# A vision tower on one core: attention steps in another order, two FFN slots interleaved, all high parts on ScalarE

## The reference

```python
    hx = _layernorm(x, ln_g, ln_b)
    q, k, v = (hx @ Wq), (hx @ Wk), (hx @ Wv)             # 2 heads of 64
    q = _l2norm(q) * scale * qn_g;  k = _l2norm(k) * scale * kn_g
    scores = jnp.einsum('bhqd,bhkd->bhqk', q, k) * dh ** (-0.5)      # causal
    attn = jax.nn.softmax(scores, axis=-1)
    y = (attn @ v) @ Wo
    gate = jax.nn.softmax(y @ gate_W + gate_b, axis=-1)
    hid = jax.nn.gelu(jnp.einsum('bnd,edf->bnef', y, W1) + b1)       # E = 8, FF = 512
    eo = jnp.einsum('bnef,efd->bned', hid, W2) + b2
    out = jnp.einsum('bned,bne->bnd', eo, gate)
```

## Time and profile before

| | |
|---|---|
| three runs, median (lowest to highest) | 1539.38 us (1537.39 to 1545.45) |
| the profiled execution | 1542.88 us, its span 1540.7 us |
| mean granted TensorE clock | 0.986 of full |
| PE busy | 1462.2 us, 95% |
| DVE busy | 1238.6 us, 80% |
| ACT busy | 1082.8 us, 70% |
| POOL busy | 329.9 us, 21% |

### The profile page before, as it was taken

One profiled execution on the slowest core, in us unless ns is written; L12 is line 12 of the kernel. 1 busy time (PEld: TensorE's weight loads), 2 busy tenths in 40 slices (PEclk: granted clock), 3 DMA queues, 4 the chain that ended last, 5 costly groups with the idle time before them and its releaser, 6 DMA issues.

```text
span 1540.7 us, 31400 instructions
## 1 busy us (share of the span) xinstructions
PE 1462.2 (95%) x10991; PEld 994.6 (65%) x10991; DVE 1238.6 (80%) x2585; ACT 1082.8 (70%) x1861; POOL 329.9 (21%) x337
## 2 busy tenths in 40 slices
PE   7898889999999999999999999999999999999998
PEld 4554556666666666666666666666666666666665
DVE  6768798878888888888888788888788888887765
ACT  5232667777777777786777777786777777777766
POOL 1135044030121313130211313130211213130101
PEclk9998899999999999999999999999999999999979
DMA  7866053333324242434233242433333242433324
GB/s 241 202 155 140 2 164 46 101 45 100 45 61 84 27 115 39 103 42 104 42 92 53 32 113 36 109 45 100 42 94 50 47 95 34 110 44 102 54 92 55
DMA packets 40340, 125.55 MB, mean 81 GB/s; under 512 B 5744, under 2 KB 5744, under 8 KB 38128
## 3 DMA queue, kind: packets, MB, share of 16 engines
q0 software_dynamic: 22464, 55.81, 25.7%
q1 hardware_dynamic: 17696, 69.28, 12.7%
q10 hardware_dynamic: 144, 0.01, 0.0%
HBM read 68.98 MB, written 50.48 MB: 78 GB/s over the span
## 4 chain that ended last, share of the span: by engine, by line
PE 59%; DVE 22%; issue 9%; ACT 7%; DMA 2%; DVEq 1%; ACTq 0%; POOLq 0%
PE pair L1009 18%; PE pair L1028 18%; PE pair L779 6%; DVE area L1434 4%; PE pair L766 4%; DVE area L1447 3%; ACT area L645 3%; PE pair L943 3%; PE pair L931 3%; DVE mx L1332 2%; ACT area L640 2%; DVE root_t L1267 2%; PE pair L807 2%; DVE area L1347 2%; PE pair L950 2%
## 5 line engine op out<-in xcount | busy, mean ns | idle before, releaser
L640 ACT ACTIVATE area<-pair,pack_b_sb 128x680 f32<-128x680 f32 x512 | 422.6, 828 | 208.1 <-PE pair L1009 206.3
L1434 DVE TENSOR_TENSOR area<-area 128x680 f16<-128x680 f32 x512 | 458.2, 898 | 128.7 <-ACT area L645 124.1
L1028 PE MATMUL pair<-area,ws 128*128 128x340 f16 x3072 | 527.9, 308 | 15.7 <-DVE area L1447 11.8
L1009 PE MATMUL pair<-area,ws 128*128 128x340 f16 x3072 | 530.2, 308 | 1.4
L1028 PEld LDWEIGHTS pair<-area,ws 128*128 128x128 f16 x3072 | 286.4, 98 | 178.9 <-DVE area L1447 44.0
L1009 PEld LDWEIGHTS pair<-area,ws 128*128 128x128 f16 x3072 | 295.3, 98 | 144.1 <-ACT area L645 3.6
L475 POOL DMA_DIRECT2D tower_out<-area x128 | 109.9, 859 | 1030.7 <-DVE area L1447 979.7
L645 ACT ACTIVATE area<-pair,pack_b_sb 128x680 f16<-128x680 f32 x384 | 316.6, 825 | 0.0
L1447 DVE SCALAR_TENSOR_TENSOR area<-pair,pack_b_sb,area 128x340 f32<-128x340 f32 x256 | 133.6, 562 | 9.4 <-PE pair L1028 9.2
L604 ACT ACTIVATE area<-pair,nbias,root 85x85 f32<-85x85 f32 (+1 forms) x256 | 112.4, 463 | 4.2 <-DVE nbias L1335 4.2
L766 PE MATMUL pair<-area,pack_a_sb 128*128 128x392 f32 (+1 forms) x260 | 92.7, 499 | 17.5 <-DVE area L1254 14.4
(11 more groups left out here) (222 smaller groups left out, 1772.8 us busy)
## 6 DMA issues: line engine op xcount, KB each, us to landing
tower_out<-area POOLq DMA_DIRECT2D x128, 340.0 KB, 4.6
area<-gate_scratch SPq DMA_DIRECT2D x16, 1360.0 KB, 10.0
area<-gate_scratch SPq DMA_DIRECT2D x16, 1020.0 KB, 7.3
area<-cells SPq DMA_DIRECT2D x16, 392.0 KB, 4.9
area<-cells POOLq DMA_DIRECT2D x14, 392.0 KB, 6.5
area<-area POOLq DMA_DIRECT2D x14, 392.0 KB, 4.3
tower_out<-ht SPq DMA_DIRECT2D x16, 340.0 KB, 2.3
area<-gate_scratch SPq DMA_DIRECT2D x16, 340.0 KB, 4.7
```

The lines of the kernel that those rows point to most:

```text
L640: nc.scalar.activation(two(hid[slot % NHID]), halves(hid_ps[slot % 2]), ACT.Gelu_apprx_tanh, bias=col(COL_B1 + slot)).then_inc(hid_ready, 1)
L1009: last = mm(hid_ps[slot % 2][:, j, 0:TH], lhs[:, w], rhs[:, j * TH:(j + 1) * TH], start=(i == 0), stop=(i == 2))
L1028: last = mm(eo_ps[:, j, 0:TH], lhs[:, w], rhs[:, j * TH:(j + 1) * TH], start=(m % CH == 0 and i == 0), stop=(m % CH == CH - 1 and i == 2))
L1434: v.tensor_tensor(hl[slot % NPART], hid[slot % NHID], hh[slot % NPART], ALU.subtract).then_inc(hlo_ready, 1)
```

## The change

- `DVE_HI = ()`: the high part of every slot is made by the second GELU pass on ScalarE. VectorE casts none. The semaphore counts follow, and TensorE's slot n + 2 now always waits for the second pass (`hidden_read`).
- FFN slots 0 and 1: their W1 matmuls are issued bank by bank, that is, logits of half 0, half 0 of slot 0, half 0 of slot 1, logits of half 1, half 1 of slot 0, half 1 of slot 1. Slot 1's own place in the order is then empty.
- Attention, VectorE: normalise 0, values 0, normalise 1, values 1, turned 0, normalise 2, turned 1, normalise 3, turned 2, turned 3.
- Attention, TensorE: channel 2 stands between the transposes of images 0 and 1, channel 3 before the transposes of image 3, and the first projection before the weighing of image 2.

```diff
+DVE_HI = ()
...
         def hi_on_act(slot):
 
-            return slot % CH > 0
+            return slot not in DVE_HI
...
+            def hidden_read(g, slot):
+
+                if hi_on_act(slot):
+                    pe.wait_ge(hhi_act, his(g, slot + 1))
+                else:
+                    pe.wait_ge(hid_ready, g * SLOTS + slot + 1)
...
                 turn_probs(g, 0)
+                graph_of(2)
                 turn_probs(g, 1)
-                graph_of(2)
                 weigh(g, 0)
                 turn_probs(g, 2)
                 weigh(g, 1)
+                graph_of(3)
                 turn_probs(g, 3)
-                graph_of(3)
+                project(g, 0)
                 weigh(g, 2)
-                project(g, 0)
                 weigh(g, 3)
...
+            def expert_half(slot, j):
+                w = slice(slot * D, (slot + 1) * D)
+                for i, (lhs, rhs) in enumerate(((w1h, yh), (w1h, yl), (w1l, yh))):
+                    last = mm(hid_ps[slot % 2][:, j, 0:TH], lhs[:, w], rhs[:, j * TH:(j + 1) * TH],
+                              start=(i == 0), stop=(i == 2))
+                return last
+
             def experts_in(g, slot):
 
-                n = g * SLOTS + slot
-                if slot >= 2 and hi_on_act(slot - 2):
-                    pe.wait_ge(hhi_act, his(g, slot - 1))
-                elif slot >= 2:
-                    pe.wait_ge(hid_ready, n - 1)
-                if slot % CH == 0:
-                    pe.wait_ge(wlo_done, 2 * (slot // CH) + 1)
-                w = slice(slot * D, (slot + 1) * D)
-                for j in range(2):
-                    if slot == 0:
+                if slot == 0:
+                    pe.wait_ge(wlo_done, 1)
+                    for j in range(2):
                         logits(g, j)
-                    for i, (lhs, rhs) in enumerate(((w1h, yh), (w1h, yl), (w1l, yh))):
-                        last = mm(hid_ps[slot % 2][:, j, 0:TH], lhs[:, w], rhs[:, j * TH:(j + 1) * TH],
-                                  start=(i == 0), stop=(i == 2))
-                last.then_inc(hid_ps_ready, 1)
+                        for n in range(2):
+                            last = expert_half(n, j)
+                            if j == 1:
+                                last.then_inc(hid_ps_ready, 1)
+                if slot >= 2:
+                    hidden_read(g, slot - 2)
+                    if slot % CH == 0:
+                        pe.wait_ge(wlo_done, 2 * (slot // CH) + 1)
+                    expert_half(slot, 0)
+                    expert_half(slot, 1).then_inc(hid_ps_ready, 1)
...
                 normalise(g, 0)
+                values_out(g, 0)
                 normalise(g, 1)
-                values_out(g, 0)
                 values_out(g, 1)
+                turned(g, 0)
                 normalise(g, 2)
-                turned(g, 0)
                 turned(g, 1)
```

More of the change, by code:

```diff
@@ L303, in hi_on_act @@
         def hi_on_act(slot):
-            return slot % CH > 0
+            return slot not in DVE_HI
         def his(g, slot):
-            return g * (SLOTS - E) + len([n for n in range(slot) if hi_on_act(n)])
+            return g * (SLOTS - len(DVE_HI)) + len([n for n in range(slot) if hi_on_act(n)])
         def steps_in(slots, slot):
@@ L906, in scores @@
                 if later:
-                    pe.wait_ge(hhi_act, his(g, 0) - 1 + m)
+                    hidden_read(g - 1, SLOTS - 2 + m)
                 elif m == 1:
@@ L1432, in experts @@
                     v.tensor_copy(hh[slot % NPART], hid[slot % NHID]).then_inc(hhi_dve, 1)
-                    dve.wait_ge(hhi_dve, g * E + slot // CH + 1)
+                    dve.wait_ge(hhi_dve, g * len(DVE_HI) + DVE_HI.index(slot) + 1)
                 v.tensor_tensor(hl[slot % NPART], hid[slot % NHID], hh[slot % NPART], ALU.subtract).then_inc(hlo_ready, 1)
```

## The result

| | before | after |
|---|---|---|
| median of the runs of this comparison | 1540.45 us | 1551.8 us (1550.74 to 1556.33, 5 runs) |
| ratio to before, 95% interval | | 1.0071 (1.0049 to 1.0092) |
| the profiled execution, its span | 1542.88, 1540.7 us | 1556.33, 1554.5 us |
| mean granted clock | 0.986 | 0.960 |
| mean of the 13 like groups (2 to 14) | 85.76 us | 86.33 us |

The change made the kernel 0.7% slower; 1.4% faster was forecast. The page shows the engine mix moving as forecast, though by less than the summed instructions (66.8 and 105.6 us): VectorE is busy 55 us less and ScalarE 85 us more. TensorE is busier by 20 us with the same 10991 matmuls. That is the first sign: the same matmuls took longer.

A forecast was written before the change was run, and what follows sets the result against it. TensorE was taken as the bound, busy 1462.2 of 1540.7 us. Like groups 10.8, slot 12 gaps 5.7, first group 1.8 and last 3 sum to 21.3: 1539.38 to 1518, range 1512 to 1525, with rivals (1) and (4) 1508 to 1532.

The forecast's parts named there:

- rival (3): TensorE's pause of about 1.1 us before slot 2 lowers its clock: +3 us, 1542 to 1600; chance 0.03.
- The interleaving: FFN slots 0 and 1 issued bank by bank: fills 0.43 us of TensorE standing, by itself worth nothing.
- The walk of waits: Both queues stepped through one steady group: attention 0.64 us earlier, new wait of 0.35 before transposes 2, slot 2 at 879.70.
- 0.77 + 0.44 = 1.21: Per like group: 0.77 us ahead by W2 slot 4, plus the 0.44 gap gone at W2 slot 12.
- First and last group: Gains outside the like groups: 1.8 us in the first (bounds 0 and 5), 3 in the last (1 and 8).
- rival (4): Last group's matmuls lose their half pace, 5 us more, and first group gives its full 5: 1510; chance 0.09.
- Rival (1): Attention wait moves to transposes 2 and mean2, losing 0.54 us per group: 1528; chance 0.22.
- Rival (2): Four GELU passes at the FFN start delay slots 2 and 3 by 0.66 us: 1545 to 1551; chance 0.04.

## Why the prediction was wrong

**The step that failed is rival (3), the clock.** It named the place, the sparse means step and the length of the pause (1.1 us; 1.13 measured), and was given 0.03; the sum of the forecast has the clock at 1.0 in every like group. Its argument against was that pauses of 0.9 us had left the clock at full, and from that it took that 1.1 would. That compares the lengths of single gaps, and two runs refute it: falls behind 0.41 us of standing, none behind 0.67 with dense matmuls ahead of it. What the runs showed in its place: 12 of 13 like groups with a stretch at half clock, and with the clock held up by idle matmuls 1523.69 us instead of 1551.8. The interleaving and the high part of slot 0 put the pause behind the thin step. Before, nine W1 matmuls stood between the long pause and the means, and slot 2 followed the means after 0.11 us (the earlier trace rows and these two of before):

```profile
877.06 1.46 PE L1009 MATMUL pair<-area,ws 128*128 128x340 f16 x9
...
878.36 1.30 PE L791 MATMUL pair<-mean_m,area 128*85 128x1 f32 x16
```

Afterwards the means were followed by 1.13 us of nothing.

Its price was right in kind. It said 2 x 0.85 = 1.7 per group; the groups at 0.98 are 1.35 to 1.4 longer than 84.65, those at 0.96 2.7. Over the 13 like groups that is 13 x (86.33 - 84.65) = 22 us. The prediction's +3 for the whole kernel came out as +11 between the medians. Between the two profiled executions it is 13.8: the 13 like groups are 7.4 longer in sum, the last but one 2.1 (84.07 against 81.93; 81.23 with the clock held up), the last 1.8, and the preparation 2.5, which the change doesn't touch.

**The walk of waits held**, in the group at exps 864.13, less 5.63. The second logits were walked as 876.71 less the 0.64 of the attention:

| | walked | measured |
|---|---|---|
| wait before transposes 2 | 0.35 | 0.40 (0.31 in the row, plus 0.1 of overlap) |
| mean2 | 872.6 | 872.69 |
| second logits | 876.07 | 876.13 |
| slot 2 | 879.70 | 879.78 |
| slot 3 | 881.13 | 882.07, at half clock |

With the clock held up the sum per like group is 85.76 - 84.66 = 1.10 us, where 0.77 + 0.44 = 1.21 was forecast. The W2 waits before slots 4 and 12 are gone: the weighting ended 29 TensorE waits of 11.8 us, and in the list of after two are left, as also with eight idle matmuls at full clock (two, 5.4 us).

```profile
PE pair L1042 <- DVE area L1461: 3.5, 2, 3.0
PE pair L1006 <- ACT area L646: 17.5, 16, 1.1
```

The second row, from the same list after, is the wait that took their place. The forecast split was off: 0.64 for the order, which gives 0.84 alone, and 0.57 for the high parts (1.21 less 0.64), which give 0.3. The interleaving gives nothing, as argued.

**First and last group.** 1.8 us were forecast for the first: it takes 94.0 us against 94.1, at a mean clock of 0.91 against 0.95, and over the 13 kernels it ranges from 89.3 at 0.98 to 96.0 at 0.91, more than the forecast gain. 3 us were forecast for the last, by less time at half clock. From its exps to the end it has 87.48 us against 85.64, with a mean clock of 0.86 against 0.88, and 85.56 in the kernel with three idle matmuls: no gain. The time at half clock stayed, so rival (4) fell too.

```profile
1467.02:1554.50 87.48, 75.62 (x504) 49.55 (x500) 49.30 (x94) 61.28 (x104) 7.75 (x9) 0.86 0.36 69
```

Rival (1) was partly there, as a wait of 0.31 for normalise 2. Rival (2), the GELU passes, was what opened the pause. In groups at full clock the pass of slot 0 costs 0.33 (84.65 against 84.33 with that slot on VectorE, neither interleaved), but all high parts on ScalarE gain 0.3 net, and alone they leave the time as it was (1.0006). The stated range ended at 1532 though rival (3) reached from 1542 to 1600; giving it 0.03 on a single observation about the clock kept it outside. The 0.05 given to a slower kernel is also less than rivals (2) and (3) have together (0.04 and 0.03), whose times are all above the kernel before. The factor of three that the prediction quotes from the Trainium skill, ScalarE: Activation LUTs, section "Rules for kernel authors", is stated there for bf16; the cast here reads fp32, and the rows have 522 ns against 825.

## What to carry to other kernels

Moving a wait is not always free; here it cost most where it landed beside thin work. When TensorE is the bound, look at what it does on both sides of the new pause, and price a half-clock stretch from the trace (here 0.5 to 2.7 us per group that has one) before the saved tenths. Read the granted clock in windows of one period before and after; equal matmul counts with more busy time are the sign. A few idle matmuls behind the thin step tell at once how much the clock takes, and the cure may then be to leave out an edit. Count falls in more than one execution before two counts are compared.

## What the hardware showed that was not expected

The length of a pause does not tell whether the clock falls. 0.72 us before the logits: none in 13 groups of before; 0.41 us behind sixteen one-column matmuls: nine of 13. The Trainium skill, TensorE: Matmul & The Clock Gate, section "A second HAM failure mode: psum-queue depth-cycling", says of one kernel that its micro-idles between groups of matmuls were frequent enough for the clock to swing between its two levels. The traces agree in that the clock goes down and up again in a group whose longest pause there is 1.13 us (0.58 and 0.56 in the two windows around the fall). Short pauses alone aren't enough here: the kernel before has several in each of its 13 like groups and no fall there.

What goes with the falls over all runs is the pause right behind the one-column matmuls: with 0.11 us there no like group has a fall (five kernels), with 0.54 to 1.26 each kernel has some, and with 0.83 but three dense matmuls ahead of it, none. That the one-column matmuls are what makes the pause harmful is the reading that fits these rows; it isn't shown, since no run moves them. How many is not a matter of the pause's length alone: 0.54 gave 4, 9 and 13.

In two kernels the groups with a fall also settle at one length. Eight groups in a row with the high part of slot 0 on VectorE took 85.27 to 85.34 us, and eleven with the order and the interleaving 85.32 to 85.36, though the first of the two needs only 84.3 without a fall. That the length settles there is seen; why, and how the number of falls depends on it, no run here shows.
